# A graph network on one core: GpSimd's gathers take their indices from the table of sources, with the first pass written out

## The reference

```python
h = jax.nn.relu(node_features @ node_proj_w.T + node_proj_b)
for l in range(L):                                  # L = 2
    trans = jnp.einsum('nh,tdh->tnd', h, edge_W[l])
    msgs = trans[edge_type, src]
    agg = jax.ops.segment_sum(msgs, dst, num_segments=num_nodes)
    h = _gru_cell(agg, h, gru_wih[l], gru_whh[l], gru_bih[l], gru_bhh[l])
    h = jax.nn.relu(h)
return h @ out_w.T + out_b                          # and x is added
```

## Time and profile before

| | |
|---|---|
| median of 3 runs | 2214.71 us (2210.9 to 2219.23) |
| the profiled execution | 2202.64 us, its span 2200.8 us |
| TensorE matmuls busy | 73% of the span |
| VectorE, ScalarE, GpSimd busy | 37%, 24%, 54% |
| mean granted TensorE clock | 0.852 of full |
| DMA | 251.55 MB, mean 114 GB/s |

### The profile page before, as it was taken

One profiled execution on the slowest core, in us unless ns is written; L12 is line 12 of the kernel. 1 busy time (PEld: TensorE's weight loads), 2 busy tenths in 40 slices (PEclk: granted clock), 3 DMA queues, 4 the chain that ended last, 5 costly groups with the idle time before them and its releaser, 6 DMA issues.

```text
span 2200.8 us, 34111 instructions
## 1 busy us (share of the span) xinstructions
PE 1611.3 (73%) x10492; PEld 1122.7 (51%) x10493; DVE 809.0 (37%) x3350; ACT 530.0 (24%) x1270; POOL 1191.4 (54%) x1282
## 2 busy tenths in 40 slices
PE   6478787777778756776766688788778775677777
PEld 4345555544444534555554455455445444555565
DVE  6564252424223243444335122221423223434443
ACT  5132232415133112222212011110413311222221
POOL 6455555555555555445542555556555555555552
PEclk9689888999889878877777888998889888888897
DMA  6325436263542322222222666674233252222221
GB/s 171 110 58 161 157 104 210 76 213 93 162 156 71 110 62 68 63 59 63 66 65 65 205 213 225 216 256 128 82 95 111 73 156 74 68 69 68 63 68 38
DMA packets 183315, 251.55 MB, mean 114 GB/s; under 512 B 24396, under 2 KB 156641, under 8 KB 183201
## 3 DMA queue, kind: packets, MB, share of 16 engines
q0 software_dynamic: 58176, 119.22, 19.5%
q1 hardware_dynamic: 123041, 130.73, 18.4%
q10 hardware_dynamic: 1984, 0.13, 0.1%
HBM read 211.87 MB, written 38.12 MB: 114 GB/s over the span
## 4 chain that ended last, share of the span: by engine, by line
PE 37%; another core or an unknown queue 29%; issue 12%; DVE 11%; ACT 3%; DMA 3%; DVEq 3%; POOL 1%; SPq 0%; PEld 0%; ACTq 0%; POOLq 0%; PEldq 0%
PE ps L1053 10%; PE ps L1124 8%; PE ps L1030 7%; PE ps L1116 5%; PE ps L991 3%; PE ps L1104 3%; DMA blocks<-node_table 2%; DVE onehot L1559 2%; DVE acc L1636 2%; ACT counts L767 1%; ACT sums_sb L833 1%; DVEq L1629 1%; DVE acc L1656 1%; DVE work L1516 1%
## 5 line engine op out<-in xcount | busy, mean ns | idle before, releaser
L595 POOL DMA_INDIRECT gath<-node_table,gidx x1212 | 1155.3, 953 | 966.8 <-ACT gidx L633 541.1
L1053 PE MATMUL ps<-counts,blocks 128*128 128x504 f16 (+3 forms) x1764 | 420.3, 385 | 77.4 <-issue 45.2
L1656 DVE TENSOR_TENSOR acc<-ps,acc 128x16 f32 x864 | 150.5, 174 | 872.0 <-PE ps L1124 400.3
L1124 PE MATMUL ps<-sums_sb,wT 128*128 128x128 f32 x1728 | 268.3, 320 | 106.7 <-ACT sums_sb L833 90.1
L833 ACT COPY sums_sb<-ps 128x512 f32<-128x512 f32 x216 | 126.7, 587 | 872.9 <-remote 552.1
L1124 PEld LDWEIGHTS ps<-sums_sb,wT 128*128 128x128 f32 x1728 | 255.6, 232 | 124.7 <-issue 63.2
L1030 PE MATMUL ps<-work 128*128 128x392 bf16 x983 | 226.5, 362 | 118.4 <-issue 46.2
L1053 PEld LDWEIGHTS ps<-counts,blocks 128*128 128x128 bf16 x1764 | 172.0, 101 | 274.4 <-issue 90.2
L1104 PE MATMUL ps<-sums_sb,wT 128*128 128x96 f32 (+1 forms) x1408 | 222.8, 313 | 90.9 <-issue 52.0
L1104 PEld LDWEIGHTS ps<-sums_sb,wT 128*128 128x128 f32 x1408 | 208.0, 226 | 119.6 <-issue 88.8
L1116 PE MATMUL ps<-onehot,gath 128*128 128x128 bf16 x2592 | 203.2, 231 | 52.3 <-issue 29.0
(11 more groups left out here) (200 smaller groups left out, 887.1 us busy)
## 6 DMA issues: line engine op xcount, KB each, us to landing
blocks<-node_table SPq DMA_DIRECT2D x84, 672.0 KB
kept_counts<-counts SPq DMA_DIRECT2D x28, 882.0 KB
counts<-kept_counts SPq DMA_DIRECT2D x28, 882.0 KB
gath<-node_table,gidx POOLq DMA_INDIRECT x1212
node_table<-gath SPq DMA_DIRECT2D x14, 336.0 KB, 3.1
node_table<-work SPq DMA_DIRECT2D x14, 336.0 KB
counts<-in_x_dram SPq DMA_DIRECT2D x1, 3080.0 KB
out_dram<-counts SPq DMA_DIRECT2D x13, 224.0 KB
```

Source lines behind the costliest of these rows:

```text
L595: nc.gpsimd.indirect_dma_start(out=gath[:, b, j, :], out_offset=None, in_=tables[l], in_offset=bass.IndirectOffsetOnAxis(ap=gidx[:, b, j:j ...
L1053: last = nc.tensor.matmul(head_ps[:, 0:COLS[share]], blocks[:, j % 2, at, part * H:(part + 1) * H], counts[:, a, 0:COLS[share]], start=(i ...
L1124: last = nc.tensor.matmul(narrow_ps[q].rearrange("p (g w) -> p g w", g=2 * BG), wT[:, W_EDGE + l * T + t, :], n_sb[:, q, :, t * NARROW:(t ...
L1656: nc.vector.tensor_tensor(win, narrow_ps[q][:, g * NARROW:(g + 1) * NARROW], win, ALU.add) \
```

## The change

`gidx` and `stage_idx` leave the first pass. A gather names its column `srcT[:, g:g + 1]` of the table directly, so the column has to be known when the program is made, and the first pass is written out, all 39 (layer 0) and 37 (layer 1) rounds. The loop, with `gidx`, stays for later passes, inside an `If`. `gathers_begun` is raised for the whole first pass at its start, and the number of passes is read after it. `typT` becomes bfloat16; `base_row` and `start_row` become partitions 0 and 32 of one tile. On ScalarE the rounds of the first pass lose `stage_idx`, and the rounds of later passes become `staged_round`, without GRU tiles.

```diff
-        typT = sb("typT", [GE, GROUPS + AHEAD])
+        typT = sb("typT", [GE, GROUPS + AHEAD], BF16)
...
-        base_row = sb("base_row", [1, GROUPS])
-        start_row = sb("start_row", [1, GROUPS], I32)
+        group_rows = sb("group_rows", [33, GROUPS])
+        base_row, start_row = group_rows[0:1, :], group_rows[32:33, :].bitcast(I32)
...
-                pool.sem_inc(es[l]["gathers_begun"], HEAD_BATCHES[l])
-
-                def gather_round(p, n, last_groups=BG):
+                def gather(index, b, j):
+                    nc.gpsimd.indirect_dma_start(
+                        out=gath[:, b, j, :], out_offset=None, in_=tables[l],
+                        in_offset=bass.IndirectOffsetOnAxis(ap=index, axis=0)).then_inc(gathered[l][b], 16)
+
+                def first_pass(n, last_groups=BG):
                     for b in range(SLOTS):
-                        k = p * BATCHES + n * SLOTS
-                        pool.wait_ge(es[l]["idx_staged"], k + (b + 1))
-                        pool.wait_ge(es[l]["sums_ready"], k + (b + 1))
-                        pool.sem_inc(es[l]["gathers_begun"], 1)
+                        pool.wait_ge(es[l]["sums_ready"], n * SLOTS + (b + 1))
                         for j in range(BG if b < SLOTS - 1 else last_groups):
-                            nc.gpsimd.indirect_dma_start(
-                                out=gath[:, b, j, :], out_offset=None, in_=tables[l],
-                                in_offset=bass.IndirectOffsetOnAxis(ap=gidx[:, b, j:j + 1], axis=0),
-                            ).then_inc(gathered[l][b], 16)
+                            g = n * ROUND + b * BG + j
+                            gather(srcT[:, g:g + 1], b, j)
...
-                gather_round(0, FIRST_ROUND[l])
-                gather_round(0, FIRST_ROUND[l] + 1)
+                pool.wait_ge(rowsT_copied, 2)
+                pool.sem_inc(es[l]["gathers_begun"], BATCHES)
+                for n in range(FIRST_ROUND[l], ROUNDS - 1):
+                    first_pass(n)
+                first_pass(ROUNDS - 1, LAST_GROUPS)
+                end_pass(0)
                 pool.wait_ge(n_pass_ready, 1)
                 n_pass = pool.value_load(passes[0:1, 1:2], min_val=1, max_val=N)
-                with pool.Fori(0, n_pass) as p:
...
+                with pool.If(n_pass > 1):
+                    with pool.Fori(1, n_pass) as p:
+                        with pool.Fori(0, ROUNDS - 1) as n:
+                            later_pass(p, n)
+                        later_pass(p, ROUNDS - 1, LAST_GROUPS)
+                        end_pass(p)
...
                 def update(b, n, begin, tile, head=None):
-                    stage_idx(l, n * ROUND + (b + SLOTS) * BG, b)
                     if head is not None:
                         head_slot(l, head + b)
...
-                with act.Fori(0, n_pass) as p:
-                    with rounds_of(act, l, p) as n:
-                        one_round(p, n)
-                    last_round(p)
+                with act.Fori(NARROW_END, ROUNDS - 1) as n:
+                    one_round(n)
+                last_round(0)
+                with act.If(n_pass > 1):
+                    with act.Fori(1, n_pass) as p:
+                        for b in range(SLOTS):
+                            stage_idx(l, b * BG, b)
+                        with act.Fori(0, ROUNDS - 1) as n:
+                            staged_round(p, n)
+                        last_round(p)
```

More of the change, by code:

```diff
@@ L704, in _ @@
             copy_rows(srcT, 6, 0)
-            act.wait_ge(ahead_copied, 1)
-            act.sem_inc(es[0]["idx_staged"], HEAD_BATCHES[0])
-            for b in range(SLOTS):
-                stage_idx(0, HEADS[0] + b * BG, b)
             act.preload_act_table(ACT.Sigmoid)
@@ L788, in _, with copy_slot, one_round, staged_round @@
                 act.sem_inc(es[l]["sums_copied"], 2 + HEAD_BATCHES[l])
-                if l > 0:
-                    act.sem_inc(es[l]["idx_staged"], HEAD_BATCHES[l])
-                    for b in range(SLOTS):
-                        stage_idx(l, HEADS[l] + b * BG, b)
-                def one_round(p, n):
+                def copy_slot(k, b):
+                    act.wait_ge(es[l]["win_done"], k + (b + 1))
+                    act.copy(s_sb[:, b % 2].rearrange("p (a g) c -> p a g c", a=2), sums[b % 2]) \
+                       .then_inc(es[l]["sums_copied"], 1)
+                def one_round(n):
                     begin, tile = round_tile(act, mybir.EngineType.Activation, n)
-                    k = p * BATCHES + n * SLOTS
+                    k = n * SLOTS
                     for b in range(SLOTS):
                         act.wait_ge(es[l]["sums_ready"], k + (b + 1 + SLOTS))
-                        act.wait_ge(es[l]["win_done"], k + (b + 1))
-                        act.copy(s_sb[:, b % 2].rearrange("p (a g) c -> p a g c", a=2), sums[b % 2]) \
-                           .then_inc(es[l]["sums_copied"], 1)
+                        copy_slot(k, b)
                         update(b, n, begin, tile)
+                def staged_round(p, n):
+                    for b in range(SLOTS):
+                        act.wait_ge(es[l]["sums_ready"], p * BATCHES + n * SLOTS + (b + 1 + SLOTS))
+                        stage_idx(l, n * ROUND + (b + SLOTS) * BG, b)
+                        copy_slot(p * BATCHES + n * SLOTS, b)
                 def last_round(p):
```

12 lines of the change are left out of this document (11 added, 1 removed).

## The result

The changed kernel took 2023.0 us (2007.7 to 2030.5), the kernel before 2213.6 in the same comparison: a ratio of 0.913 [0.907, 0.918]. Two more comparisons gave 2029.2 and 2026.3 us, 0.919 [0.913, 0.924] and 0.922 [0.915, 0.928]. The profiled executions, 2202.6 and 2030.5 us, are 172.1 apart, and it is these 172 us that the rows have to explain.

What follows compares the result with a forecast made beforehand. Rows of gathers and the pauses in which TensorE's late signals get through were taken to bound the kernel; 2202.6 - 39 - 3 + 1 + 1 = 2162.6, plus 12.1 to the median, gave 2174.7 us, range 2100 to 2255.

Steps and rivals of the forecast that it cites:

- the way from signal to gather: GpSimd's wait before a row of gathers: without the index copy, each such wait gets 0.77 us shorter.
- What bounds the kernel: Layer 1's rounds: TensorE's signals arrive late during rows of gathers, get through in pauses of 3.0 to 3.4 us.
- Its own 0.84 from signal to gather stays: GpSimd's start after the index copy: the 0.84 us delay was taken to remain once the copy is gone.
- I take three quarters: Layer 1: of 52 us from 68 shorter waits, 39 us reach the end, since TensorE is busy 78% of the head.
- For layer 0 ... I take nothing: Layer 0's rounds: no gain, because ScalarE's casts of counts and the gates set the rounds more.
- much faster: Rival: layer 0 profits as well, 119 us from 154 waits and 3 from ScalarE, 2093 us; chance 12%.
- Straight code, tiles: GpSimd's written-out pass costs 1 us of fetching; bfloat16 types cost 1 us, start_row's move to partition 32 nothing.
- ScalarE's relief: ScalarE's 312 index copies leave the first pass: 3 us gained, bounds 0 and 8.
- The rows of gathers join: Slower rival on GpSimd: rows of eight become twelve or sixteen, 3.7 us a joined round, 2259 us for 12; chance 26%.
- sign of "slower": VectorE's waits for the unknown releaser growing past 291.5 us would show that rows of gathers had joined.

Runs made afterwards that it cites:

- idx_first: The kernel before with ScalarE's index copy moved ahead of its wait for win_done and its copy of the sums: 2168.5 us, 0.984 of the kernel before.
- delay_02: The changed kernel with a 0.87 us GpSimd fill ahead of the gathers of slots 0 and 2: 1741.7 us beside 1637.3 for the kernel before, 2062.7 beside 2204.9.

## Why the prediction fell short

The step that failed is the size of the gain in two terms of the sum: layer 0, taken at nothing, gave 110 us, and the way from signal to gather, taken at 0.77 us shorter, became 1.28 us shorter.

- *What bounds the kernel*: right in the main. Along a row of gathers TensorE's signals reach the others ever later (3.97 us in the round shown after the change, 0.04 with fills instead of gathers). That they only get through in the pause is too strong: beside the first two gathers of a row nine in ten come on time. A shorter wait of GpSimd makes the run shorter (`idx_first`) and a longer one makes it longer (`delay_02`), though in these two by a half and a third of its size, so the pace isn't that of row and pause alone.
- *"After: the gather waits only for the sums ... Its own 0.84 from signal to gather stays"*: wrong. The 0.84 us were the hop from ScalarE to GpSimd, which goes with the copy. TensorE's signal reaches both engines at nearly the same moment, so the gather starts 0.24 us after ScalarE instead of 1.52: 1.28 us less, not 0.77. `idx_first`, which keeps the hop, gave 38 us.
- *"I take three quarters"*: about right in layer 1. In the three steps shown from its head the pause became 1.1 us shorter and the step 1.15, but its gathers as a whole took 65 us less, where its 71 waits by 1.28 us are 91: 0.72. The reason that I gave, a TensorE busy for 78% of the head, no run tested. The forecast for layer 1, 39 us, was short by the price of a wait.
- *"For layer 0 ... I take nothing"*: wrong by the most, 110 us. Its 83 waits by 1.28 us are 106. Its longer idle times before gathers (5.79 and 5.78 us in the earlier trace rows) I had read as ScalarE's gates being the limit; they are 1.83 to 3.21 us now, and its wide rounds lost 4.9 us each. That ScalarE's other work ahead of the index copy made them long, so that they had more to lose, is what I take from this, and no run took it by itself.
- With 1.28 us for all 154 waits the same sum would have been 197 us with full pass-through in both layers and 148 with three quarters, against 172 in the profiled executions and 190 in the medians. That it falls between is partly luck, since a wait in layer 0's wide rounds lost more than 1.28 us, and the clock has no term in it. The rival "much faster" had the place right and the price wrong (119 us), and its 12% were too few.
- *Straight code, tiles*: right, 0.998 each. *ScalarE's relief*, 3 us taken, 8 as the bound: 0 to 20 us by the runs, not settled.
- *The rows of gathers join*: it did not happen. The reason that I gave against it held: a gather still needs a signal of TensorE. The rows became shorter: counted from GpSimd's timeline with a new row wherever two starts are over 1.9 us apart, there were 78 of four, 54 of eight and 27 of twelve before, 130, 61 and 13 after. My price of 3.7 us a round was for rounds that also had other work, and it was never measured. VectorE's largest wait for the unknown releaser grew all the same, from 291.5 to 338.4 us; as a sign of "slower" it was useless:

```profile
DVE acc L1673 <- remote: 338.4, 36, 16.5
```

## What to carry to other kernels

When a wait goes through a second engine, its price is measured from the moment the second engine hears its signal to the moment the waiting one starts (here 1.52 us), not by the copy in between (0.20); the hop goes with the copy. Where the cadence is "row of work, pause", a saving in the pause is worth something in every stage that has the pause, also where nothing waits for the data; a stage is not put at nothing without a row of its own. How much of a pause is passed on has to be measured: it was 0.72 in layer 1 here, about a half with `idx_first` and a third with `delay_02`. And before a gain is promised elsewhere, the kernel's own time has to be seen in more than one set: here one program had two paces, 2205 and 1640 us, and the gain was measured at one of them.

## What the hardware showed

- With rows of gathers on GpSimd about a third of TensorE's signals came over 1 us after the modelled end of their matmuls (379 of 1167), few beside the first two gathers of a row (25 of 273) and most from the fifth on (197 of 223). With fills of 1.02 us in place of the gathers 7 of 1245 did. A third of the bytes or half the rows left it as it was (407 of 1067, 390 of 1100). VectorE's and ScalarE's signals were on time throughout (under 1%).
- The kernel before took 2205 us in three sets of runs and 1640 in two. `delay_02`, traced in a set of each kind, had gathers of 955 and 956 ns in both; in the quick one the signals were on time although gathers ran without a pause. What decides between them is open.
- An indirect gather cost GpSimd 949 ns with 256 bytes a row and 909 ns with 64 rows instead of 128, beside 952 ns in full.
- VectorE's busy time rose from 809.0 to 859.9 us with fills on GpSimd, with the same 3350 instructions. With all the gathers it was 809.0, with half of them 804.9.
